# Attention on one core: V products of a quarter in two halves of 256 queries, a maximum product between them

## What is computed

```python
q, k, v = (proj(w_q), proj(w_k), proj(w_v))
scores = jnp.einsum('bhqd,bhkd->bhqk', q, k) / jnp.sqrt(jnp.float32(D_K))
attn = jax.nn.softmax(scores, axis=-1)
out = jnp.einsum('bhqk,bhkd->bhqd', attn, v)
...
x = x + _L0_attn_ref(_layernorm(x, axis=-1), ...)
x = x + _L0_ffn_ref(_layernorm(x, axis=-1), ...)
```

## Time and profile before

| | |
|---|---|
| median of 3 runs | 563.24 us (562.98 to 564.12) |
| the profiled execution | 562.15 us, span of the core 560.3 us |
| PE busy | 537.7 us, 96% of the span |
| DVE busy | 386.5 us, 69% |
| ACT busy | 324.6 us, 58% |
| mean granted clock of PE | 0.989 of full speed |

### The profile page before, as it was taken

How to read it: one execution, slowest core, us unless ns; L and a number is a source line. 1 busy time by engine, 2 the same in 40 slices (tenths; PEclk the granted TensorE clock), 3 DMA queues, 4 the chain that set the end, 5 groups by cost and what they waited for, 6 DMA issues and landing times.

```text
span 560.3 us, 9693 instructions
## 1 busy us (share of the span) xinstructions
PE 537.7 (96%) x3504; PEld 391.4 (70%) x3504; DVE 386.5 (69%) x706; ACT 324.6 (58%) x480; POOL 116.2 (21%) x145
## 2 busy tenths in 40 slices
PE   8999999899999999999999989999999999999991
PEld 6887665333333333333778979999999999999980
DVE  6914657889998999961688986755728375667650
ACT  4322115767878777878345463746657475757540
POOL 3400111002022020622001203234341321241212
PEclk9999999999999999999998999999999999999996
DMA  8390368937465753004464599583764757586112
GB/s 329 103 112 2 56 83 98 114 47 89 70 97 76 92 75 99 12 19 165 156 223 134 185 352 329 145 309 51 287 153 154 267 144 278 117 299 160 32 30 37
DMA packets 29068, 78.19 MB, mean 140 GB/s; under 512 B 7644, under 2 KB 8924, under 8 KB 24538
## 3 DMA queue, kind: packets, MB, share of 16 engines
q1 hardware_dynamic: 23722, 68.84, 47.0%
q0 software_dynamic: 5296, 8.69, 8.4%
HBM read 53.11 MB, written 9.32 MB: 111 GB/s over the span
## 4 chain that ended last, share of the span: by engine, by line
PE 77%; DVE 13%; issue 3%; DMA 2%; ACT 2%; POOL 1%; SPq 0%; POOLq 0%; DVEq 0%; ACTq 0%
PE ps L728 15%; PE ps L729 14%; PE ps L730 14%; PE ps_o L740 8%; DVE neg_max L1466 8%; PE ps L759 6%; PE ps L771 4%; PE ps_m L759 3%; PE ps L796 2%; DVE w_lo L1575 1%; DMA w_sb<-w 1%; PE ps L777 1%; PE ps_o L728 1%; PE ps_m L728 1%; PE ps_m L1022 1%
## 5 line engine op out<-in xcount | busy, mean ns | idle before, releaser
L1251 ACT ACTIVATE probs_t<-ps 128x1024 f32<-128x1024 f32 x128 | 124.2, 1022 | 32.9 <-PE ps L771 32.3
L1466 DVE TENSOR_REDUCE neg_max<-ps 128x1 f32<-128x512 f32 x170 | 111.8, 685 | 14.7 <-PE ps L759 12.1
L728 PE MATMUL ps<-xgT_hi,w_hi 128*128 128x256 f32 (+7 forms) x380 | 109.5, 288 | 1.0 <-DVE xgT_lo L1732 1.0
L729 PE MATMUL ps<-xgT_lo,w_hi 128*128 128x256 f32 (+7 forms) x380 | 108.5, 286 | 0.0
L730 PE MATMUL ps<-xgT_hi,w_lo 128*128 128x256 f32 (+7 forms) x380 | 108.5, 286 | 0.0
L759 PE MATMUL ps<-k_stack,q_stack 48*128 48x512 f32 x170 | 70.3, 456 | 3.8 <-issue 1.7
L728 PEld LDWEIGHTS ps<-xgT_hi,w_hi 128*128 128x128 f32 x380 | 72.0, 189 | 1.3 <-DVE xgT_lo L1732 1.1
L729 PEld LDWEIGHTS ps<-xgT_lo,w_hi 128*128 128x128 f32 x380 | 72.0, 189 | 0.1
L730 PEld LDWEIGHTS ps<-xgT_hi,w_lo 128*128 128x128 f32 x380 | 71.9, 189 | 0.0
L740 PE MATMUL ps_o<-probs_t,v_ones 128*32 128x512 f32 x512 | 68.1, 605 | 0.0
L1749 DVE TENSOR_TENSOR act<-gate,ps 128x256 f32<-128x256 f32 (+7 forms) x48 | 20.7, 430 | 67.8 <-PE ps L730 53.5
(11 more groups left out here) (329 smaller groups left out, 982.2 us busy)
## 6 DMA issues: line engine op xcount, KB each, us to landing
w_sb<-w SPq DMA_DIRECT2D x16, 1024.0 KB
w_sb<-w SPq DMA_DIRECT2D x8, 1536.0 KB
w_sb<-w SPq DMA_DIRECT2D x8, 1152.0 KB
q_stack<-q_hi SPq DMA_DIRECT2D x32, 128.0 KB, 5.4
k_stack<-k_hi SPq DMA_DIRECT2D x32, 128.0 KB, 5.1
q_stack<-q_lo SPq DMA_DIRECT2D x16, 128.0 KB, 4.7
k_stack<-k_lo SPq DMA_DIRECT2D x16, 128.0 KB, 5.9
q_hi<-o_raw SPq DMA_DIRECT2D x16, 128.0 KB, 4.7
```

The costliest lines, as they stand in the source:

```text
L728: pe.matmul(o, x_hi, w_hi, start=start, stop=False)
L729: pe.matmul(o, x_hi, w_lo, start=False, stop=False)
L1251: a.activation(probs_t[:, kc % 2, 2 * half:2 * half + 2, :], ps4[:, 2 * (n % 2):2 * (n % 2) + 2, :], ACT.Exp, scale=D ** -0.5).then_inc(s_ ...
L1466: v.tensor_reduce(neg_max[:, g % 2, col:col + 1], max_bank(g, u2), AX.X, ALU.max, negate=True).then_inc(s_mx, 1)
```

## The change

In every step with an `a` other than the first two (b = 0 and 1, which also carry a part of the V projection), the V product is issued in two halves: the four heads' products with queries 0 to 255, then maximum product 1, then the four heads' products with queries 256 to 511. These are 54 steps. The steps without an `a` keep one V product over all 512 queries. The waits stand ahead of the first half, and `s_pv` is counted by the second. Only the very first product into a head's partitions of the bank carries the start flag, so that the second half of a group's first quarter adds with `start=False`.

```diff
-            def pv(g, kc):
+            def pv(g, kc, q0, q1):
 
                 if not 0 <= g < NG:
                     return
-                pe.wait_ge(s_ex, UNITS * g + 2 * (kc + 1))
-                if kc == 0 and g >= 1:
-                    pe.wait_ge(s_or, g)
+                if q0 == 0:
+                    pe.wait_ge(s_ex, UNITS * g + 2 * (kc + 1))
+                    if kc == 0 and g >= 1:
+                        pe.wait_ge(s_or, g)
                 for j in range(GH):
-                    last = pe.matmul(ps_o[32 * j:32 * j + 32, :],
+                    last = pe.matmul(ps_o[32 * j:32 * j + 32, q0:q1],
                                      v_ones[:, (g // 8) * TPB + kc, (g % 8) * GH + j, :, :].rearrange("p d o -> p (d o)"),
-                                     probs_t[:, kc % 2, j, :], start=(kc == 0), stop=(kc == TPB - 1),
-                                     tile_position=(0, 32 * j))
-                last.then_inc(s_pv, 1)
+                                     probs_t[:, kc % 2, j, q0:q1], start=(kc == q0 == 0), stop=(kc == TPB - 1 and q1 == S),
+                                     tile_position=(0, 32 * j), skip_group_check=True)
+                if q1 == S:
+                    last.then_inc(s_pv, 1)
...
                 key_max(ga, 4 * pa)
-                key_max(ga, 4 * pa + 1)
                 if b == 0:
+                    key_max(ga, 4 * pa + 1)
                     pe.wait_ge(s_ja, a_count[n_of["v", 1, TPB - 2]])
-                if b == 1:
+                elif b == 1:
+                    key_max(ga, 4 * pa + 1)
                     v_tail(ps_o[:, :], TPB - 1, HC // 2, HC).then_inc(s_job, 1)
-                if (group, kc) == (0, 0):
-                    pe.wait_ge(s_ja, a_count[-1])
-                pv(group, kc)
+                elif ga < NG:
+                    if (group, kc) == (0, 0):
+                        pe.wait_ge(s_ja, a_count[-1])
+                    pv(group, kc, 0, S // 2)
+                    key_max(ga, 4 * pa + 1)
+                    pv(group, kc, S // 2, S)
+                else:
+                    pv(group, kc, 0, S)
                 key_max(ga, 4 * pa + 2)
```

## The result

The changed kernel takes 569.85 us in the median against 563.11 us, a ratio of 1.0114 (95% interval 1.0095 to 1.0134): 1.1% slower. The sign and the range of the prediction hold; the size does not: +6.7 us where +3.1 was forecast. The ratio above rests on three executions of the changed kernel and four of the kernel before.

What follows compares the result with a forecast made beforehand. It took a ring through PE and DVE, neither alone, as the bound. A block becomes 6 x 2.67 + 2 x 3.13 + 0.30 = 22.58 against 22.07; six blocks add 3.1: 566.3 us, range 561.0 to 572.0.

Steps and rivals of the forecast that it cites:

- The loop through both engines: Before the change: reduction 2, product 1, V product, product 2 and its reduction, across PE and DVE; 2.69 us per step.
- PE's own path: What PE alone needs in a plain step: 2.33 us before, 2.67 after, when it would take the lead.
- plain step: Step without transposition or shuffle: 2.69 us before, forecast 2.67 after, a gain of 0.02.
- A half: V product over 256 queries, start to next product: forecast 0.56 us, bounds 0.50 and 0.66.
- the passage between products: From product 1's start to the second V half's start: forecast 0.42 us, bounds 0.32 and 0.52.
- Rival C: Much slower: a half keeps more fixed cost; 571 us at 0.61 a half, 576 at 0.66; chance 0.10.
- Rival A: Faster: products 1 and 2 load weights under the halves, PE's path 2.47 us, total 557.8; chance 0.15.
- B: No measurable change: half 0.02 to 0.03 cheaper, shuffle absorbed, block 22.1 to 22.2, 563.2 to 564.3 us; chance 0.13.
- The step with a transposition: PE needs 0.46 us more there, formerly hidden by float: 2.77 us before, forecast 3.13 after.
- the float: PE's slack per step before the change, 0.36 us, forecast to be gone after it.
- the ring: The loop through PE and DVE via the maximum products' banks; forecast to fall to 2.52 us a step.
- The shuffle: Keeps DVE 0.64 us in one step per block; forecast 0.30 over a plain step, between nothing and 0.37.

Runs made afterwards that it cites:

- e4: Kernel before with reductions over 256 of 512 keys, exponentials scaled by a further quarter; ran once, 636.88 us, only its attention stage read.
- e3: Changed kernel with reductions over 256 of 512 keys, exponentials scaled by a further quarter; ran once, 749.92 us, only its attention stage read.
- e1: Changed kernel with the two V halves back to back, both maximum products ahead of them; 565.21 us, 1.0016 of the kernel before.
- x3: Changed kernel with maximum products 1 and 2 side by side between the halves, from b = 16 on only; 559.41 us, 0.9943 of the kernel before.
- a1: The changed kernel run again, unedited, beside the kernel before; median 591.07 us (569.02 to 613.04), ratio 1.0108.
- x1: Changed kernel with both maximum products ahead of the first half, second half behind product 3, in plain steps only; 574.24 us.
- x2: Changed kernel with maximum products 1 and 2 side by side between the halves in all changed steps; 562.41 us, 1.0008 of the kernel before.
- e5: Changed kernel, but steps with a transposition and two whose successor lacks maximum products keep the old order; 570.8 us, 1.0121 of the kernel before.
- e2: Changed kernel with the V product whole again and maximum product 1 behind it; 570.3 us, 1.0146 of the kernel before.

## Why the prediction was right in sign and wrong in size

**Right: what bounds.** The loop through both engines set the step before (e4), PE's own path sets the plain step after (e3). The halving costs nearly nothing by itself (e1). A half lasts 0.57 for 0.56 forecast, the passage between products 0.43 for 0.42. Rival C did not come: its halves of over 0.6 are not there. Rival A did not come either: the second half stands 0.43 behind product 1 and not 0.33, and a plain step takes 2.70, not 2.47. Nor did B: the block is 23.11, not 22.1 to 22.2. The Trainium skill, "TensorEngine Tiling (Array Packing)", Key Properties, says that a change of tiling mode drains the engine; the 0.43 agree with it as far as a distance between starts can show it.

**Wrong: sizes, in four terms.** The largest miss comes from a wait that the prediction left out. A block of eight steps grew by 1.04 where the working said 0.51, and six blocks make 6.2 for 3.1. That the measured time lies within the forecast's range is owed to its width of 561 to 572 us and not to the account of what grows.

- *The step with a transposition* was put at 3.13 and takes 3.28: twice 0.15 in a block, over half of the miss. The step that failed is "With the float gone it lasts 2.67 + 0.46 = 3.13", together with "no wait for DVE" ahead of product 0. It adds up PE's path alone and asks the ring nothing. From product 2 to the next half the prediction's own terms of the ring give 0.52 + 0.75 + 0.42 = 1.69, and those of PE 0.42 + 0.85 + 0.32 = 1.59; the larger would have counted. Measured are 0.53 + 0.75 + 0.43 = 1.71, and 0.43 + 0.78 + 0.33 = 1.54 for PE's own (e3); the 0.17 between them is the wait. Its term 0.85, "from there to product 0 of the next step", was taken as PE's own and was the ring's already in the kernel before: reduction 2 began at 207.29 and ended at 207.98, and product 0 began 0.06 later. The number came out right, 0.85 again, for the wrong reason; with it the 0.32 behind product 0 became 0.43, since a product that waited stands alone. I had the ring for plain steps and forgot that the transposition takes a turn in it.
- *The shuffle* was put at 0.30 over a plain step, with 0.37 as its upper bound; it is 0.35.
- *The plain step* was put at 2.67 and takes 2.70: halves of 0.57 and passages of 0.43. The gain of 0.02 a step is gone, and the five plain steps of a block and the shuffle's at 0.03 more are the rest of its miss.
- *Two steps that I counted as plain.* The steps at a = 28 and 55 have a successor without maximum products, so the ring did not bound them before; they lasted 1.90 and 2.06 us and now last 2.48 and 2.64 (at a = 28 the V products start at 168.00 and 169.91 before, at 171.74 and 174.21 after): 1.2 us more in all.

The first six changed steps took 0.5 more, as forecast, and PE's wait for the stack shrank from 1.73 to 1.06; but the stack came 0.4 us later in this execution. In every profiled execution that ran at full clock up to there, the V product of the step at a = 8 begins 17.7 to 18.1 us after the first V product, whatever the steps before it took. So the stage grew by 6.2 + 1.2 + 0.4 = 7.8 us between the profiled executions, which is the span's growth; the first transfer of x took 0.8 longer in the later one, and about as much came back behind the stage. The medians differ by 6.7 because the profiled execution of before lay 1.1 under its median.

## What to carry to other kernels

Before giving a stall's time to a change, write down the loop that makes it, with each wait, and then the path of the engine that will lead next, and compare the two in every kind of step; a distance between two starts is an engine's own only if no wait ends right ahead of the second. Check the loop for the rare members of a step as well (a transposition that takes a turn in the ring, a step without a successor), since an order that is neutral in the usual step can lose all its gain there. If a block must be cut, put into the cut what can share one passage: two products between the halves gained 0.6% on the kernel before (x3) where one lost 1.1%.

## What the runs showed of the hardware

- The 128x32 products start 0.43 us behind a lone 48x128 product and 0.33 behind one in a stream. The other way, the next product starts 0.52 us after the start of the last of the 128x32 products over 512 columns (206.25 to 206.77 before) and 0.31 after the last over 256 (203.47 to 203.78 after). The two rounds of four such products start 0.43 us apart for 512 columns and 0.22 for 256, so the change of shape takes about 0.09 beyond the round.
- The granted clock can stay at 1.2 GHz for 102 us of unbroken work, after an idle wait of 1.1 us in the same place where other executions of the same kernel kept 2.4 GHz. Of the orders tried, those with V halves and one product between showed the longest spells behind a wait (a1 102 us, e3 239 us); x1 had 27, e1 and x2 10, e4 and e5 3 us, and the profiles of before, after, e2 and x3 none in the stage, after idle waits of 1.73, 1.06, 1.03 and 1.72 us. Each is one profiled execution. What in the order decides how long a spell lasts was not settled.
